# Five of seven layer-0 tiles in three rounded passes, and the layout steps of a chunk two groups later, in a DLRM/CIN tower on one core

## The reference

```python
def _cin_layer(X0, Xi, W, b):
    H = W.shape[0]
    Wr = W.reshape(H, X0.shape[1], Xi.shape[1])
    return jnp.einsum('hjk,bjd,bkd->bhd', Wr, X0, Xi) + b[None, :, None]
Xi = X0                       # (512, 39, 16), gathered
for W, b in Ws:               # three layers of 128 outputs
    Xi = _cin_layer(X0, Xi, W, b)
    res.append(Xi.sum(axis=2))
h = concat(res, dense_ctx)    # (512, 400)
h = relu(h @ W_top1 + b_top1); h = relu(h @ W_top2 + b_top2)
y = h @ W_top3
```

## Time and profile before

| | us |
|---|---|
| median of 3 runs (lowest to highest) | 679.53 (679.16 to 680.07) |
| the profiled execution, its own time | 680.41 |
| its span | 678.6 |
| start of a chunk's (3,1) layer-0 tile to that of the next, in the steady part | 36.72 |
| TensorE busy in the span | 643.5 (95%) |
| VectorE, ScalarE, GpSimd busy | 577.1, 514.1, 346.2 |

### The profile page before, as it was taken

One profiled execution on the slowest core, in us unless ns is written; L12 is line 12 of the kernel. 1 busy time (PEld: TensorE's weight loads), 2 busy tenths in 40 slices (PEclk: granted clock), 3 DMA queues, 4 the chain that ended last, 5 costly groups with the idle time before them and its releaser, 6 DMA issues.

```text
span 678.6 us, 13696 instructions
## 1 busy us (share of the span) xinstructions
PE 643.5 (95%) x2521; PEld 460.9 (68%) x2521; DVE 577.1 (85%) x1240; ACT 514.1 (76%) x1676; POOL 346.2 (51%) x339
## 2 busy tenths in 40 slices
PE   0389999999999999999999999999999999999998
PEld 0157777677777777777777777777777777767483
DVE  0448898989899999989898989899998989999580
ACT  2147878788787878787878878787878787899382
POOL 6768483838474665647383847465562333220000
PEclk9989999999999999999999999999999999999999
DMA  7532722131221303031212122130303030000100
GB/s 219 129 74 60 254 45 88 43 89 42 63 67 45 87 15 97 22 95 37 88 43 89 42 74 56 50 81 20 95 20 102 24 92 25 13 15 2 62 1 0
DMA packets 40878, 43.57 MB, mean 64 GB/s; under 512 B 20288, under 2 KB 23744, under 8 KB 40713
## 3 DMA queue, kind: packets, MB, share of 16 engines
q1 hardware_dynamic: 24482, 39.73, 19.5%
q0 software_dynamic: 5120, 1.32, 2.2%
q10 hardware_dynamic: 11239, 2.05, 1.6%
HBM read 41.75 MB, written 1.31 MB: 63 GB/s over the span
## 4 chain that ended last, share of the span: by engine, by line
PE 83%; issue 8%; DVE 4%; POOL 2%; SPq 2%; ACT 0%; DVEq 0%; DMA 0%; ACTq 0%; POOLq 0%
PE acc L410 13%; PE ya L433 11%; PE ya L434 11%; PE ya L435 11%; PE yd L433 9%; PE yd L435 8%; PE yd L434 8%; PE misc L417 5%; DVE chain L554 2%; PE yd L505 2%; POOL emb L336 1%; PE misc L403 1%; SPq L254 1%; POOL prod L264 1%; PE yd L512 1%
## 5 line engine op out<-in xcount | busy, mean ns | idle before, releaser
L679 ACT ACTIVATE prods<-ya,x0t 128x128 f32<-128x128 f32 x1472 | 442.3, 502 | 103.3 <-PE ya L435 68.8
L554 DVE SCALAR_TENSOR_TENSOR chain<-yd,x0t,chain 128x128 f32<-128x128 f32 x768 | 217.8, 342 | 18.4 <-PE yd L435 17.8
L433 PE MATMUL ya<-w1h,x1h 128*128 128x512 f32 (+1 forms) x384 | 206.4, 537 | 1.9 <-DVE x1l L573 1.9
L264 POOL TENSOR_TENSOR prod<-tiles,x0a 120x512 f32<-120x512 f32 x105 | 137.4, 1309 | 130.6 <-PE acc L410 117.7
L336 POOL DMA_INDIRECT emb<-in_tables,rows x160 | 158.4, 990 | 39.4 <-issue 32.2
L434 PE MATMUL ya<-w1l,x1h 128*128 128x512 f32 (+1 forms) x384 | 147.8, 385 | 0.0
L435 PE MATMUL ya<-w1h,x1l 128*128 128x512 f32 (+1 forms) x384 | 147.7, 385 | 0.0
L569 DVE TENSOR_REDUCE x2t<-prods 128x128 f32<-128x1792 f32 x64 | 129.2, 2019 | 1.5 <-DVE chain L554 0.3
L410 PE MATMUL acc<-prod,w 120*128 120x512 f32 x224 | 116.9, 608 | 0.5 <-POOL prod L264 0.5
L569 DVE TENSOR_REDUCE prods<-prods 128x128 f32<-128x1536 f32 x64 | 111.7, 1745 | 0.0
L433 PE MATMUL yd<-w1h,x1h 128*128 128x512 f32 x256 | 104.7, 409 | 2.4 <-DVE chain L554 1.3
(11 more groups left out here) (85 smaller groups left out, 413.1 us busy)
## 6 DMA issues: line engine op xcount, KB each, us to landing
tiles<-x_rows SPq DMA_DIRECT2D x236, 78.0 KB
x0a<-x_rows SPq DMA_DIRECT2D x45, 80.0 KB
emb<-in_tables,rows POOLq DMA_INDIRECT x160
w<-in_w SPq DMA_DIRECT2D x3, 832.0 KB
w<-in_w SPq DMA_DIRECT2D x1, 2496.0 KB, 9.1
tiles<-x_rows SPq DMA_DIRECT2D x32, 42.0 KB
x<-x_rows SPq DMA_DIRECT2D x16, 78.0 KB
tiles<-x_rows SPq DMA_DIRECT2D x15, 72.0 KB
```

The lines of the kernel that those rows point to most:

```text
L264: engine.tensor_tensor(prod0[:, i % L0_PRODS, :], tiles[:, slot, :], x0a[:, :], ALU.mult).then_inc(prod0_ready, 1)
L433: pe.matmul(out, x1h[:, xs], w1h[:, cols], start=True, stop=False)
L554: dve.scalar_tensor_tensor(out, product, x, run if step else b1[:, :], ALU.mult, ALU.add).then_inc(yd_used, 1)
L679: mm = act.activation(prods[:, :, slot_of(q) + i], ya[(NA * g + k) % YA][:, i * H:(i + 1) * H], ACT.Copy, scale=turned(c)[:, g * F1 + j:g ...
```

## The change

Tiles 0 to 4 of the chunks 2 to 15 run as three rounded passes. The high part of `w0` is rounded once by ScalarE and its low part taken by VectorE, before chunk 0. For each such tile ScalarE rounds the product to `prod0h` (`round_product`, placed by `HIGH_AFTER`: tile 0 after (3,4) of the chunk before, tiles 1 to 4 after (0,0), (0,5), (1,0), (1,5)), and GpSimd subtracts to get `prod0l` (`split_product`, in its queue behind the next product). There are two buffers each, and a product's buffer is now free when GpSimd has split it.

`lay_out` stands after (2,1) and `turn_x0` after (3,1) in all chunks. The gathers are spread (1, 1, 1, 1, 1, 2, 3 behind the seven products) and the block diagonals stand behind products 1, 3, 5 and 6, the last one behind the gathers. For three groups of x1 VectorE now computes `x1l` from the bank `acc0` with the bias and `x1h` in one instruction, not from `x1`. `stack` and `y` have no memory of their own any more. SP's queue is as it was.

```diff
-DIAG_AFTER = {0: 0, 2: 1, 4: 2, 6: 3}
+DIAG_AFTER = {1: 0, 3: 1, 5: 2, 6: 3}
+GATHERS_AFTER = (1, 1, 1, 1, 1, 2, 3)
+SPLIT, SPLIT_FROM = (0, 1, 2, 3, 4), 2
+HIGH_AFTER = {0: (3, 4), 1: (0, 0), 2: (0, 5), 3: (1, 0), 4: (1, 5)}
 def lay_after(prev):
-    return (0, 1) if prev else (2, 1)
+    return (2, 1)
 def turn_after(prev):
-    return (2, 1) if prev else (3, 1)
+    return (3, 1)
...
+def products_free(x, i):
+    if i >= L0_PRODS:
+        px, pi = x, i - L0_PRODS
+    else:
+        px, pi = x - 1, range(i, T0, L0_PRODS)[-1]
+    if px >= SPLIT_FROM and pi in SPLIT:
+        return "split", splits_before(px, SPLIT.index(pi)) + 1
+    return "plain", T0 * px + pi + 1
...
+            def split_product(x, i):      # GpSimd
+                k = SPLIT.index(i)
+                pool.wait_ge(prod0_high, splits_before(x, k) + 1)
+                pool.wait_ge(prod0_ready, T0 * x + i + 1)
+                wait_done(pool, l0_done, halves_free(x, i))
+                pool.tensor_tensor(prod0l[:, k % L0_PRODS, :], prod0[:, i % L0_PRODS, :],
+                                   prod0h[:, k % L0_PRODS, :].bitcast(F32), ALU.subtract).then_inc(prod0_split, 1)
...
                     if c + 1 < CHUNKS:
                         multiply0(pool, c + 1, i)
-                    if i in DIAG_AFTER:
+                        if c + 1 >= SPLIT_FROM and i - 1 in SPLIT:
+                            split_product(c + 1, i - 1)
+                    if i in DIAG_AFTER and i < T0 - 1:
                         block_diagonal(c, DIAG_AFTER[i])
-                    if c + 3 < CHUNKS and 2 * i < FO:
-                        gather(c + 3, range(2 * i, 2 * i + 2))
+                    if c + 3 < CHUNKS:
+                        gather(c + 3, range(sum(GATHERS_AFTER[:i]), sum(GATHERS_AFTER[:i + 1])))
+                    if i == T0 - 1:
+                        block_diagonal(c, DIAG_AFTER[i])
...
+                if x >= SPLIT_FROM and i in SPLIT:      # TensorE, layer0
+                    pe.wait_ge(prod0_split, splits_before(x, k) + 1)
+                    pe.matmul(acc0[:, :], w0h[:, k, :], high, start=first, stop=False)
+                    pe.matmul(acc0[:, :], w0l[:, k, :], high, start=False, stop=False)
+                    pe.matmul(acc0[:, :], w0h[:, k, :], low, start=False, stop=last).then_inc(l0_done, 1)
...
+            def split_front(c):           # VectorE
+                dve.wait_ge(x1h_front, c + 1)
+                groups = acc0[:, :].rearrange("p (n g) -> p g n", g=GROUPS)[:, 0:GROUPS - 1, :]
+                dve.scalar_tensor_tensor(x1l[:, FRONT].rearrange("p (g n) -> p g n", n=P), groups, bias[:, 0:1],
+                                         x1h[:, FRONT].bitcast(F32).rearrange("p (g n) -> p g n", n=P),
+                                         ALU.add, ALU.subtract).then_inc(x1_front, 1)
...
+            def round_product(x, i):      # ScalarE
+                k = SPLIT.index(i)
+                act.wait_ge(prod0_ready, T0 * x + i + 1)
+                wait_done(act, l0_done, halves_free(x, i))
+                act.activation(prod0h[:, k % L0_PRODS, :], prod0[:, i % L0_PRODS, :], ACT.Copy).then_inc(prod0_high, 1)
...
+                        for i in SPLIT:
+                            if (g, q) == HIGH_AFTER[i] and (lay if i == 0 else prev and nxt):
+                                round_product(c + 1 + (i == 0), i)
```

More of the change, by code:

```diff
@@ L75 @@
 G_AFTER, TURN_1 = 6, (0, 8)
-DIAG_AFTER = {0: 0, 2: 1, 4: 2, 6: 3}
+DIAG_AFTER = {1: 0, 3: 1, 5: 2, 6: 3}
+GATHERS_AFTER = (1, 1, 1, 1, 1, 2, 3)
+SPLIT, SPLIT_FROM = (0, 1, 2, 3, 4), 2
+HIGH_AFTER = {0: (3, 4), 1: (0, 0), 2: (0, 5), 3: (1, 0), 4: (1, 5)}
+assert sum(GATHERS_AFTER) == FO
 def lay_after(prev):
-    return (0, 1) if prev else (2, 1)
+    return (2, 1)
 def turn_after(prev):
-    return (2, 1) if prev else (3, 1)
+    return (3, 1)
 def segments(i):
@@ L109, in uses_before, with splits_before, halves_free @@
     return 0 if isinstance(x, int) and x == 0 else T0 * (x - 1) + range(i, T0, ring)[-1] + 1
+def splits_before(x, k):
+    return len(SPLIT) * (x - SPLIT_FROM) + k
+def products_free(x, i):
[6 more added lines that the diff above has]
+    return "plain", T0 * px + pi + 1
+def halves_free(x, i):
+    k = SPLIT.index(i)
+    if k >= L0_PRODS:
+        return T0 * x + SPLIT[k - L0_PRODS] + 1
+    return T0 * (x - 1) + SPLIT[range(k, len(SPLIT), L0_PRODS)[-1]] + 1
 def wait_done(engine, semaphore, count):
@@ L262, in multiply0 @@
             engine.wait_ge(tile_in[slot], 16 * SEGMENTS * (x * len(range(slot, T0, L0_TILES)) + i // L0_TILES + 1))
-            wait_done(engine, l0_done, uses_before(i, L0_PRODS, x))
+            kind, count = products_free(x, i)
+            wait_done(engine, prod0_split if kind == "split" else l0_done, count)
             engine.tensor_tensor(prod0[:, i % L0_PRODS, :], tiles[:, slot, :], x0a[:, :],
@@ L326, in _ @@
             sp.wait_ge(tail_act, 8)
-            sp.dma_start(a["out"].rearrange("b o -> o b"), y[:, :]).then_inc(out_done, 16)
+            sp.dma_start(a["out"].rearrange("b o -> o b"), y).then_inc(out_done, 16)
             sp.wait_ge(out_done, 16)
@@ L406, in layer0 @@
             def layer0(x, i):
-                pe.wait_ge(prod0_ready, T0 * x + i + 1)
-                if i == 0:
+                first, last = i == 0, i == T0 - 1
+                if first:
                     wait_done(pe, x1_ready, x)
-                pe.matmul(acc0[:, :], w0[:, i, :], prod0[:, i % L0_PRODS, :],
-                          start=(i == 0), stop=(i == T0 - 1)).then_inc(l0_done, 1)
+                if x >= SPLIT_FROM and i in SPLIT:
+                    k = SPLIT.index(i)
+                    high, low = prod0h[:, k % L0_PRODS, :], prod0l[:, k % L0_PRODS, :]
+                    pe.wait_ge(prod0_split, splits_before(x, k) + 1)
+                    pe.matmul(acc0[:, :], w0h[:, k, :], high, start=first, stop=False)
+                    pe.matmul(acc0[:, :], w0l[:, k, :], high, start=False, stop=False)
+                    pe.matmul(acc0[:, :], w0h[:, k, :], low, start=False, stop=last).then_inc(l0_done, 1)
+                else:
+                    pe.wait_ge(prod0_ready, T0 * x + i + 1)
+                    pe.matmul(acc0[:, :], w0[:, i, :], prod0[:, i % L0_PRODS, :],
+                              start=first, stop=last).then_inc(l0_done, 1)
             def gram_group(n, g):
@@ L477, in _ @@
             lay_out(1)
+            pe.wait_ge(w0_split, 1)
             pe.wait_ge(w1_split, W1_PARTS)
```

25 lines of the change are left out of this document (18 added, 7 removed).

## The result

The changed kernel took 727.67 us (median of 4 runs, 720.42 to 735.36) against 679.53: a ratio of 1.067, interval 1.063 to 1.073. One of the four, the 735.36, was a slow execution, and the ratio is taken without it. The forecast was 688.3, with a range from 670 to 697. The profiled execution took 727.98 us, its span is 726.2.

A forecast was written before the change was run, and what follows sets the result against it. TensorE bounds the kernel; a loop through the (3,1) wait takes 26.85 + 0.4 + 10.1 = 37.35 us against 36.72. Twelve periods give +7.6, with one-offs +8.8, on 679.5: 688.3, range 670 to 697.

The forecast's parts named there:

- What they cost elsewhere: Split work on other engines: ScalarE's roundings 3.2 us a chunk, GpSimd's subtractions 6.5, to 28.3 busy, all hidden.
- Split tiles: TensorE's layer-0 tiles: 0.68 us split against 0.88 plain; 0.18 taken a tile, 0.9 a chunk, 12.6 over 14 chunks.
- ScalarE: Five roundings of 631 ns, 33.2 us busy, under a chunk; as rival bound, about 38.0 a chunk, 697, chance 0.05.
- VectorE's front `x1l`: VectorE's new `x1l` instruction reading PSUM: 0.6 us, bounds 0.5 and 0.8, where the old one took 548 ns.
- The path to (3,1): Layout at (2,1) to the seventh tile's matmul: 10.1 us, bounds 9.9 and 10.9, against TensorE's 9.07; wait 1.0.
- Start of chunk 1: First product for chunk 2 late behind the load of w2; split ready at 85.3, wanted at 83.1: +2.2 us.
- Chunk 0: The 0.54 us stall goes, since five fewer gathers stand ahead of that product: -0.6 us.
- The clock rival: Clock halves behind each (3,1) wait for 3.5 us, 1.7 lost each, 22 on top of 688: 710; chance 0.07.
- VectorE gives back 0.4: Turn before (3,3) delays VectorE, so TensorE waits for banks in groups 0 and 1: 0.4 us, bounds 0 and 0.7.
- the mechanism that was forecast: TensorE waits 1.0 us at (3,1) in chunks 1 to 13 for the late product; period 37.35 against 36.72.

The follow-up runs named there:

- e10: The changed kernel with the fourth group's `x1l` computed in half 0 of group 2 instead of group 0: 690.96 us, ratio 1.017.
- e4: The kernel before with only the layout moved to (2,1) and the turn to (3,1) in all chunks: 693.18 us, ratio 1.022.
- e8: The kernel before with two extra GpSimd additions behind the second product in chunks 1 to 12: 691.43 us, ratio 1.019.
- e1: The changed kernel with the fourth group's `x1l` also taken from the PSUM bank; TensorE waits for it: 702.54 us, ratio 1.035.
- e15: The changed kernel with old layout and turn places, fourth-group `x1l` in half 1 of group 2, splits from chunk 3 on: 670.81 us, ratio 0.989.
- e2: The changed kernel with SP's load of the seventh tile ahead of the x0 load: 685.44 us, ratio 1.008.
- e5: The changed kernel with the layout back at (0,1) and the turn back at (2,1): 687.96 us, ratio 1.012.
- e7: The changed kernel with GpSimd's gather put between each product and the subtraction behind it: 705.15 us, ratio 1.037.
- e9: The kernel before with two extra one-input GpSimd copies behind the second product in chunks 1 to 12, single run: 680.1 us.
- e11: As e10, with the layout back at (0,1) and the turn at (2,1): 679.73 us, ratio 1.000 to the kernel before.
- e12: As e10, with SP loading the seventh tile ahead of x0: 679.49 us, ratio 1.000 to the kernel before.
- e13: As e12, with the fourth group's `x1l` in half 1 of group 2: 675.32 us, ratio 0.994 to the kernel before.
- e3: The changed kernel with both the fourth group's `x1l` from the bank and the seventh tile loaded ahead of x0: 687.93 us, ratio 1.012.

## Why the prediction was wrong

The step that failed is under "What they cost elsewhere": GpSimd's five subtractions, "6.5 us, 21.8 + 6.5 = 28.3, hidden too". A subtraction was priced by GpSimd's own time, and its cost to VectorE was put at nothing without a reason. GpSimd did take 27.8 us a chunk and did have its splits ready, but its time was not free for VectorE. I costed its instructions by what waits for their results, and never asked what runs beside them. What stood in its place: in ten of twelve periods VectorE's fourth-group `x1l` lasted 2.56 to 3.15 us and not 0.28, behind a product and a subtraction of GpSimd, TensorE waited 2.14 to 2.73 us for what follows it, and a period was 41.2 and not 37.35. The range missed for the same reason: no rival held a collision between VectorE and GpSimd.

- *The size of it.* Ten of twelve periods at 41.2 instead of 37.4 are +39 us; e10, which only moves `x1l` away, measures 36.7. e4 and e8 show both halves: the move with one collision instead of ten costs 13.7 us, a shorter collision without the move about 1 us a chunk.
- *The rule that was left out.* The Trainium skill has it (SBUF — State Buffer, section Who interferes with whom): a VectorE instruction with two SBUF inputs and a GpSimd instruction that reads SBUF cannot run together, and whichever came first holds the shared pair to its end. The runs agree that they do not run together, the PSUM form's 0.34 us in e1 included, and add that two GpSimd instructions back to back hold VectorE through both (2.87 us). They do not bear out who goes first, at least not by the starts on record: in five of the ten disturbed chunks `x1l` starts ahead of the product, by up to 0.45 us, and is held all the same.
- *Why it did not hurt before.* In chunks 2 to 12 of the kernel before a gather stood beside this `x1l`, with another gather behind it, and in the last three GpSimd stood still (0.28 us each time). The subtractions and the later seventh product moved GpSimd's queue against VectorE's until a product and a subtraction stood there. In e4, without subtractions, a product did in one chunk.
- *Split tiles.* Right: 322.98 to 323.67 in the changed kernel is 0.69 for three passes, forecast 0.68.
- *ScalarE.* Roundings took 678 ns, forecast 631; 32.1 busy, forecast 33.2. Not the bound.
- *VectorE's front `x1l`.* 608 ns, forecast 0.6.
- *The path to (3,1).* Right in form and nearly in size: from layout to product end 302.19 to 312.02 are 9.8 us (forecast 10.1), copy to x0 load 2.71 (2.93; the median of the 13 stretches it was taken from is 2.97), wait 0.53 to 1.00 (1.0). From the end of the last tile issue to the product are 1.78 us, 308.95 to 310.73, where chunk 0 had 1.94; so the 2.0 us that the forecast took from the Trainium skill for its estimate come out too long here (the section named there is on DMAs that GpSimd issues, and these are SyncE's). Undisturbed periods are 37.37 and 37.54 (37.35). The path is not steady, though: in e10 it was 2 us longer in two of thirteen chunks.
- *Start of chunk 1.* Under-sized: 3.25 us of wait where 2.2 was forecast, and for a bank that ScalarE holds, not for the split tile itself; then 5.9 us at half clock behind it (79.80 to 85.70), another 2.9.

```profile
80.00:85.70 5.70, 5.70 (x14) 4.44 (x15) 3.38 (x6) 5.14 (x19) 5.52 (x6) 0.50 0.19 52
```

- *Chunk 0.* Its gain was under-sized too, and this paid for the start of chunk 1: the seventh tile runs at 67.36 against 72.54, -5.2 where I had -0.6. TensorE begins at 38.34 against 40.16; the half clock that the kernel before had from 41.05 for 3.4 us (1.7 us of work) does not come; and two waits are gone, the 0.54 of the earlier trace rows and one of 0.73 at 48.22. The first two are not shown to be the change's doing: over all the traces chunk 0 begins between 37.9 and 40.9, and of the four traces without split tiles one (e4) lacks the half clock too.
- *The clock rival.* Its place was wrong and its mechanism right. The clock did not fall behind a wait of up to 1.00 us at (3,1), but it did behind eight of the ten Gram waits, of 2.14 to 2.73 us; the length does not decide, since behind waits of 2.70 and 2.24 it stayed. In e10 it fell at (3,1) itself, behind one wait of 2.48, and not behind one of 2.71. A wait that lowers the clock in trip after trip is what the Trainium skill describes (TensorE: Matmul & The Clock Gate, section HAM oscillation), and the trace agrees for these eight.
- *VectorE gives back 0.4.* About right: TensorE waits 0.20 for VectorE's bank at (0,3) in most chunks, and in e15, without any other wait, a period is 36.25 and not 35.8.

So the mechanism that was forecast was in the kernel and cost nearly what was said (37.25 a period in nine of e10's twelve, against 37.35). The larger one was missed.

## What to carry to other kernels

When work goes to GpSimd, list what VectorE runs at the same time, and mark each instruction that has both inputs in SBUF. An unedited instruction whose mean rises several times is the place to look, above its waits. An operation that is not needed soon can be put where GpSimd is idle, or in a gather with no product right behind it; here that alone was worth 37 us of 727, and with it the split tiles pay (e15, 1.1% under the kernel before).

## What the runs showed of the hardware

A 128x128 subtraction of VectorE with two SBUF inputs, once it is held, ends 0.15 to 0.18 us after the GpSimd instruction that holds it (e2, e4, e5, e7 to e9, e11, e12 and the changed kernel), whether that multiplies, adds, subtracts or copies. It is held through two in a row. A gather alone does not hold it (0.28 at 244.79), but one that began in the gather and 0.43 us ahead of the product behind it was held through that product (chunk 3, 3.12 us). There is a form in between: in e13 to e15 it begins 0.1 to 0.3 us ahead of a diagonal of GpSimd and takes 0.39 to 0.56 us (once 1.16), and the diagonal beside it about 0.84 instead of 0.73. The same subtraction with one input in PSUM took 0.34 to 0.35 us in every chunk of e1 and e3, in e3 with GpSimd's subtraction running beside it (120.30 to 121.58, `x1l` at 120.68). TensorE's granted clock fell to half behind waits of 3.25 us (for 5.9 us) and 2.46 us (for 3.4 us), stayed at 1.00 behind one of 2.70 in the same kernel and one of 3.33 in e7, and was 1.00 behind all of 0.5 to 1.0. Behind the wait of 1.9 us before chunk 0 it fell in some executions and not in others.
